# Three cross attentions: softmax sums written once, reciprocals spread by DMA, maxima in bf16 parts, loads moved

## The chip, the core and the metric

The kernel runs on one core of a Trainium2 chip. The time is device microseconds for one execution of the whole program; the number compared is the median of several executions. The engines are TensorE (PE in the profile; PEld is its weight load), VectorE (DVE), ScalarE (ACT), GpSimd (POOL) and SyncE (SP, which here only waits and starts DMAs). They run their own instruction streams and meet at semaphores.

## The reference

Four layers of a gated model on x of 8 batches x 512 tokens x 256 channels. Each layer adds a cross attention to a context of 64 tokens per batch, then another block:

```
x = x + tanh(g_xattn[i]) * cross_attention_i(layernorm(x), ctx)     # i = 0..3
x = x + tanh(g_ffn[i])   * block_i(layernorm(x))                    # local/routed attention, int8 MLP, gated unit, 8-expert MoE
```

Layers 0, 1 and 3 have a cross attention with 16 heads of 16 channels, and these three share one piece of code:

```
q = xn @ Wq + bq ; k = ctx @ Wk + bk ; v = ctx @ Wv + bv            # layer 0 rotates q and k by position
s = q k^T * scale, masked ; s = s - max(s) ; p = exp(s)
o = (p v) / sum(p) ; y = o @ Wo + bo
```

All data are fp32. Layer 2's cross attention has code of its own and isn't touched.

## The kernel before

The program is a sequence of eight stages (`L0_xattn`, `L0_ffn`, `L1_xattn`, ... `L3_ffn`). x stays in SBUF (`x_all`). Weights of the next stage are loaded by SP's queue when a stage begins: the block at `@block.sync` waits until the stage before has updated x, then starts every pair of `later.loads` (L383), then runs `early_sync_program` and the stage's own `sync_program`. The order of each engine's work is written out by hand, in `xattn_pe`, `xattn_act`, `xattn_dve` and `xattn_pool`; there is no planner.

A cross attention is a pipeline over turns n = 0, 1, ..., each holding pieces of several batches: scores of batch n, softmax of n-1, output of n-2 (`turn_of`), and in L3 also the routing for the last stage, for n-3 and n-4. Each piece is done in two halves f = 0, 1, of 8 heads. One batch of 512 queries is four tiles of 128 (t).

- `scores(n, f)` (PE, L621 for the mask, L627) writes query-major scores into banks 0 to 3; `maxima` (DVE, L1143) reduces them to 32 numbers per query row.
- `turn_max(n)` (PE, L639) transposes the maxima of a batch, in four fp32 transposes, into bank 6 (L0, L1) or 5 (L3); ACT copies them to `maxT` (`copy_max`, L905). Because bank 6 also takes the output projection, `project_out(n-2, 2)` waits for that copy.
- `scores_of_keys(n-1, f)` (PE) computes the scores again, key-major (L647), and subtracts the maxima by a matmul with a constant `minus_max` (L650), fp32; ACT takes the exponentials (`exponentials`, L901).
- `values` (PE, L660) multiplies by v into bank 4. `denominators` (PE, L671) multiplies the same exponentials by the constant `sums`: four matmuls with 32-column weights side by side (column groups), 512 columns each, into bank 5. Every sum is written 16 times, once for each channel of its head, so that it lies where the output lies.
- `normalise` (DVE) takes the reciprocal of bank 5 (L1148, 128 x 512), then multiplies bank 4 by it into `o` (L1151). `values` of the next half waits for that, as it reuses bank 4.
- `project_out` (PE, L677) and `add_out` (DVE, L1158) put the result into x.
- L0 also rotates: `partners` (PE, L608) and `rotate` (DVE, L1131, L1135, L1138). `banks_free` on PE waits until `rotate` has read its two products.

DVE's order in a turn is: maxima(n, 0); normalise(n-2, 1); statistics of later batches in turns 0 to 2; maxima(n, 1); rotate(n+1) in L0; normalise(n-1, 0); apply(n+2) (layer norm); expert choice in L3; add_out(n-2). L1 also dequantises the next stage's weights on DVE in turns 4 and 5, and runs its first layer norms in turns 7 and 8. A turn counts as steady where all pieces are present.

SP in L0 stores rows for the next stage (`units_sync`), one batch a turn, and reloads one block of them into `xn` after the third. In L3 the last 24 indirect scatters on POOL come after the loop, and the first tile of the last stage waits for all of them.

## Time and profile before

| | us |
|---|---|
| median of 3 executions | 2500.14 (2499.08 to 2505.13) |
| profiled execution | 2494.2 |
| its span, first to last instruction | 2492.2 |
| PE busy | 2329.9 |
| DVE busy | 1410.5 |
| ACT busy | 950.6 |
| POOL busy | 613.6 |

The three stages run at about 0 to 236 us (L0), 975 to 1173 us (L1) and 1660 to 1926 us (L3). Busy time is the union of an engine's instructions; matmul ends are modelled, so distances between starts are the safer measure on PE. An fp32 matmul is two records in the trace. PEclk is the granted share of TensorE's full clock. A row of windows gives the stretch and its length, then the busy time (and number of instructions) of PE, PEld, DVE, ACT and POOL, then PEclk, the mean busy share of the DMA engines, and GB/s; with a source line it has PE and PEld only. A row of groups by line ends with busy time (union) and mean ns of one instruction.

### The profile page before, as it was taken

What the parts mean: (1) busy time and instruction counts of PE and PEld (TensorE: products, weight loads), DVE (VectorE), ACT (ScalarE), POOL (GpSimd) and SP (SyncE); (2) the same over time, 40 slices, a digit from 0 to 9 for tenths busy, and PEclk for the clock granted to TensorE, in tenths of its full rate; (3) what the DMA queues carried; (4) which work ended last, traced back from release to release, by engine and by line L of the source; (5) the groups of instructions that cost most, each with busy time, mean ns of one, the idle gap of its engine ahead of it and who ended that gap; (6) DMA issues with size and microseconds to landing.
All of it is one profiled execution on the core that took longest, in us unless ns stands there. A gap on an engine that the chain in (4) does not pass through costs nothing.

```text
span 2492.2 us, 40543 instructions
## 1 busy us (share of the span) xinstructions
PE 2329.9 (93%) x15438; PEld 1656.4 (66%) x15438; DVE 1410.5 (57%) x2881; ACT 950.6 (38%) x2288; POOL 613.6 (25%) x548
## 2 busy tenths in 40 slices
PE   6997999999999998998999999988984999999998
PEld 4444677776666665444666665544553999999997
DVE  7886654674544555887466533348885444444442
ACT  1366655444444543332233322124653222222222
POOL 3234222252001002211233100014455122222222
PEclk8998999999999999999999999989996999999999
DMA  5011211121001000100001029502126222222221
GB/s 202 1 35 51 91 35 52 52 83 54 26 26 52 26 26 26 71 1 18 1 1 36 1 95 326 185 0 110 40 80 244 58 36 37 35 36 36 36 35 26
DMA packets 72087, 148.36 MB, mean 60 GB/s; under 512 B 11704, under 2 KB 59065, under 8 KB 69441
## 3 DMA queue, kind: packets, MB, share of 16 engines
q1 hardware_dynamic: 39600, 104.61, 12.3%
q0 software_dynamic: 16368, 26.23, 5.4%
q10 hardware_dynamic: 15936, 15.03, 2.1%
q8 instruction: 122, 2.00, 0.3%
q14 instruction: 61, 0.49, 0.1%
HBM read 107.42 MB, written 74.76 MB: 73 GB/s over the span
## 4 chain that ended last, share of the span: by engine, by line
PE 81%; DVE 10%; ACT 4%; issue 2%; POOL 2%; DMA 1%; SPq 0%; DVEq 0%; POOLq 0%; ACTq 0%
PE PS L2366 14%; PE PS L2392 7%; PE PS L2822 5%; PE PS L2834 5%; PE PS L1540 4%; PE PS L1531 4%; PE PS L2050 3%; PE PS L2062 3%; PE PS L2891 3%; PE PS L602 3%; PE PS L2882 3%; PE PS L2856 3%; DVE mem L1148 2%; DVE mem L1143 2%; PE PS L2927 2%
## 5 line engine op out<-in xcount | busy, mean ns | idle before, releaser
L2366 PEld LDWEIGHTS PS<-ctx2T,x_all 128*128 128x128 f32 x3124 | 361.2, 193 | 10.1 <-DVE x_all L2515 6.5
L2366 PE MATMUL PS<-ctx2T,x_all 128*128 128x128 f32 x3124 | 361.8, 276 | 5.9 <-DVE x_all L2515 5.1
L2563 POOL DMA_INDIRECT out_x<-xnT,moe_small x71 | 130.9, 1843 | 427.7 <-ACT xnT L2448 424.7
L2392 PE MATMUL PS<-mem,moe_small 128*128 x852 | 195.8, 379 | 0.8 <-ACT xnT L2448 0.8
L2515 DVE COPY x_all<-mem 128x2816 f32 x71 | 115.5, 1627 | 109.6 <-issue 96.9
L2392 PEld LDWEIGHTS PS<-mem,moe_small 128*128 128x128 f32 x852 | 156.4, 190 | 19.4 <-issue 1.2
L1148 DVE RECIPROCAL mem<-PS 128x512 f32<-128x512 f32 x48 | 160.9, 3351 | 11.3 <-PE PS L671 11.0
L1143 DVE TENSOR_REDUCE mem<-PS 128x32 f32<-128x2048 f32 x48 | 109.9, 2289 | 50.8 <-PE PS L627 50.7
L3208 DVE TENSOR_REDUCE moe_small<-PS 128x2 f32<-128x1024 f32 x64 | 78.5, 1226 | 99.2 <-PE PS L2882 99.2
L3353 POOL TENSOR_TENSOR mem<-mem,moe_small 128x512 f32<-128x512 f32 x64 | 82.2, 1304 | 207.5 <-DVE moe_small L3218 207.4
L3032 ACT ACTIVATE mem<-PS,moe_small 128x128 f32<-128x128 f32 x256 | 89.9, 377 | 94.2 <-DVE moe_small L3203 94.2
L2891 PEld LDWEIGHTS PS<-consts,mem 128*128 128x128 f32 x768 | 87.8, 141 | 54.3 <-issue 52.4
L3041 ACT ACTIVATE mem<-PS,moe_small 128x512 f32<-128x512 f32 x128 | 86.9, 690 | 85.0 <-DVE moe_small L3208 85.0
L677 PE MATMUL PS<-mem 128*128 128x256 f32 x384 | 100.5, 407 | 19.7 <-DVE mem L1151 12.5
L1540 PE MATMUL PS<-mem 128*128 128x256 f32 x512 | 116.6, 381 | 0.0
L2528 DVE TENSOR_TENSOR moe_small<-PS,moe_small 128x128 f32<-128x128 f32 x71 | 20.7, 292 | 167.1 <-ACT moe_small L2441 167.1
L2782 POOL DMA_INDIRECT mem<-routed_out,moe_small x32 | 30.8, 962 | 342.1 <-DMA routed_out<-mem 334.6
L1531 PE MATMUL PS<-mem 128*128 128x512 f32 x256 | 113.9, 594 | 0.0
L901 ACT ACTIVATE mem<-PS,mem 128x2048 f32<-128x2048 f32 x32 | 63.0, 1967 | 117.6 <-PE PS L650 117.6
L1540 PEld LDWEIGHTS PS<-mem 128*128 128x128 f32 x512 | 95.5, 190 | 18.5 <-issue 7.0
L677 PEld LDWEIGHTS PS<-mem 128*128 128x128 f32 x384 | 73.8, 203 | 44.4 <-issue 23.3
L2891 PE MATMUL PS<-consts,mem 128*128 128x128 f32 x768 | 101.1, 275 | 0.9 <-DVE mem L3226 0.9
(382 smaller groups left out, 4596.9 us busy)
## 6 DMA issues: line engine op xcount, KB each, us to landing
slots<-in_trash_rows SPq DMA_DIRECT2D x8, 4290.0 KB, 63.8
mem<-in_L_ffn_experts SPq DMA_DIRECT2D x8, 2176.0 KB, 13.6
xn<-slots ACTq DMA_DIRECT2D x53, 130.0 KB, 2.1
x_all<-in_x SPq DMA_DIRECT2D x8, 512.0 KB, 8.1
xn<-unit_rows SPq DMA_DIRECT2D x8, 512.0 KB, 4.5
mem<-unit_rows SPq DMA_DIRECT2D x8, 512.0 KB, 4.3
out_x<-x_all ACTq DMA_DIRECT2D x8, 512.0 KB, 2.9
unit_rows<-moe_small SPq DMA_DIRECT2D x7, 512.0 KB, 3.2
```

The source lines that it names most:

```text
L677: last = nc.tensor.matmul(PS[:, BANK_M + 1 - t // 2, (t % 2) * D:(t % 2 + 1) * D], s.o[:, b % 2, f, t * P:(t + 1) * P], s.wo[:, f, :], sta ...
L1143: dve.tensor_reduce(s.max.rearrange("p (g n) -> p g n", g=G)[:, :, 8 * f:8 * f + 8], PS[:, 0:G, :].rearrange("p g (a k) -> p g a k", k=SC) ...
L1148: dve.reciprocal(s.recip, PS[:, BANK_DEN, :]).then_inc(s.sems["recip_ready"], 1)
L1531: last = nc.tensor.matmul(PS[:, 2 + n % 2, :], s.w1[:, k, n * P:(n + 1) * P], s.hT[:, k, :], start=k == 0, stop=k == KD - 1)
L1540: last = nc.tensor.matmul(PS[:, 6 + t % 2, 0:D], s.yT[:, n, t * P:(t + 1) * P], s.w2[:, n, :], start=n == 0, stop=n == KF - 1)
L2366: last = nc.tensor.matmul(PS[:, moe_bank(j, part), c * P:(c + 1) * P], m.w[:, j % 2, k, at:at + P], m.rowT[:, j % 2, k, :], start=k == 0, ...
L2392: last = nc.tensor.matmul(PS[:, MOE_BANK_Y, 0:D], m.hT[:, j % 2, n, :], w[:, :, at:at + D], start=n == 0, stop=n == KE - 1)
L2515: dve.tensor_copy(m.w[:, j % 2, :, :].rearrange("p k n -> p (k n)"), s.experts[:, bass.ds(expert, 1), 0:KD * WIDE].rearrange("p o n -> p ( ...
L2563: nc.gpsimd.indirect_dma_start(s.T["out"], bass.IndirectOffsetOnAxis(s.token[:, j % 4:j % 4 + 1], 0), m.result[:, j % 4, :], None, compute ...
L2822: last = nc.tensor.matmul(PS[:, BANK[p.heavy, "k", j], :], s.wk[p.heavy][:, k, m * P:(m + 1) * P], columns(p, j)[:, k, :], start=k == 0, s ...
L2834: last = nc.tensor.matmul(PS[:, BANK[p.heavy, "v", j], t * P:(t + 1) * P], columns(p, j)[:, k, t * P:(t + 1) * P], s.wv[p.heavy][:, k, m * ...
L2891: last = nc.tensor.transpose(PS[:, BANK_PT + h, n * P:(n + 1) * P], s.probs[:, par, h, n * P:(n + 1) * P], e.ident)
```

## The change

1. `denominators`: for all batches but the last, a sum is written for each query tile t into one of the 16 rows of its head, over 128 columns instead of 512. That takes 16 matmuls of 128 columns with the constants `sums_of_tile[:, t, :]`, accumulating over t. The reciprocal is then 128 x 128. The last batch keeps the old form.
2. SP stores these reciprocals to DRAM (128 rows of 512 bytes), waits for the store, and reads them back broadcast: each of the 16 rows of a head gets the head's 512 numbers, into `s.recip`. One buffer serves all halves, so each read waits for the product before it.
3. ACT copies the values' bank to `o` (`copy_o`, two a turn), and DVE multiplies `o` in place one slot later: half 0 after the next turn's first maxima, half 1 after its second maxima. `values` of the next half now waits for ACT's copy.
4. The maxima are split by DVE into three bf16 parts (`split_max`, four operations on 64 elements per row), transposed in bf16 into bank 4, copied as bf16, and subtracted by bf16 matmuls with 12 rows of `minus_max`. The projection no longer waits for that copy, and its tiles stand together around `turn_max`.
5. Loads: in L1 ACT starts the next stage's loads, in turns 2 to 5; in L3 SP starts two experts' loads and a third one after the last reciprocals; in L0 ACT stores the unit rows and SP reloads `xn` after the last reciprocals. DVE's dequantisation in L1 moves to turns 6 and 7. In L0 POOL adds the bias ahead of scaling the next stage's weights.

```diff
+def split_max(eng, order, s, b):
+    eng.wait_ge(s.sems["max_ready"], 2 * (b + 1))
+    order.mark(eng.tensor_copy(max_part(s, 0), s.max))
+    order.settle()
+    order.mark(eng.tensor_tensor(s.max_rest, s.max, max_part(s, 0), ALU.subtract))
+    order.settle()
+    order.mark(eng.tensor_copy(max_part(s, 1), s.max_rest))
+    order.settle()
+    eng.tensor_tensor(max_part(s, 2), s.max_rest, max_part(s, 1), ALU.subtract).then_inc(s.sems["max_split"], 1)
+
+def spread_recips(sp, s, b, f):
+    k = KD * b + f
+    few = s.recips[f].rearrange("(q r) n -> q r n", r=HD)[:, 0:TB, :].rearrange("q t n -> q (t n)").rearrange("q (o n) -> q o n", o=1)
+    sp.wait_ge(s.sems["recip_ready"], k + 1)
+    sp.dma_start(s.recips[f], s.recip_few).then_inc(s.sems["recip_stored"], 16)
+    sp.wait_ge(s.sems["recip_stored"], 16 * (k + 1))
+    wait_for(sp, s.sems["o_ready"], k)
+    sp.dma_start(s.recip, few.broadcast_to([NH // KD, HD, S])).then_inc(s.sems["recip_spread"], 16)
+
+def recips_sync(sp, e, s):
+    for b in range(B - 1):
+        for f in range(KD):
+            spread_recips(sp, s, b, f)
+    if s.late_loads:
+        for dst, src in s.next.loads:
+            sp.dma_start(dst, src).then_inc(s.next.weights_loaded, 16)
+        sp.dma_start(*s.next.expert_loads[5]).then_inc(s.next.expert_loaded_s[3], 16)
...
     def turn_max(b):
-        pe.wait_ge(s.sems["max_ready"], 2 * (b + 1))
+        pe.wait_ge(s.sems["max_split"], b + 1)
+        if b == 0:
+            pe.wait_ge(s.sems["v_ready"], B)
+        else:
+            pe.wait_ge(s.sems["o_copied"], KD * (b - 1) + 1)
...
     def values(b, f):
-        wait_for(pe, s.sems["o_ready"], KD * b + f)
+        wait_for(pe, s.sems["o_copied"], KD * b + f)
+        if f == 1:
+            pe.wait_ge(s.sems["maxT_ready"], min(b + 2, B))
...
     def denominators(b, f):
+        if b == B - 1:
...
+        else:
+            for t in range(TB):
+                for c in range(G):
+                    last = nc.tensor.matmul(PS[c * GR:(c + 1) * GR, BANK_DEN, 0:P], s.sums_of_tile[:, t, :],
+                                            s.probsT[:, f, c, t * P:(t + 1) * P], start=t == 0, stop=t == TB - 1)
...
-            if old and not s.front:
-                project_out(n - 2, 0)
         if before:
             scores_of_keys(n - 1, 1, min(2 * n + 2, 2 * B))
         if s.rope:
             banks_free()
         if route:
             logits(n - 3)
-        if old and s.front:
+        if old:
             project_out(n - 2, 0)
+            project_out(n - 2, 1)
         if now:
             turn_max(n)
...
+    def copy_o(b, f):
+        act.wait_ge(s.sems["pv_psum"], KD * b + f + 1)
+        wait_for(act, s.sems["y_psum"], 2 * (b - 1))
+        nc.scalar.activation(s.o[:, b % 2, f, :], PS[:, BANK_O, :], ACT.Copy).then_inc(s.sems["o_copied"], 1)
...
+    def reciprocals(b, f):
+        dve.wait_ge(s.sems["den_psum"], KD * b + f + 1)
+        if b == B - 1:
+            dve.wait_ge(s.sems["o_ready"], KD * b + f)
+            dve.reciprocal(s.recip, PS[:, BANK_DEN, :]).then_inc(s.sems["recip_ready"], 1)
+        else:
+            wait_for(dve, s.sems["recip_stored"], 16 * (KD * b + f))
+            dve.reciprocal(s.recip_few, PS[:, BANK_DEN, 0:P]).then_inc(s.sems["recip_ready"], 1)
...
     def normalise(b, f):
-        dve.tensor_tensor(s.o[:, b % 2, f, :], PS[:, BANK_O, :], s.recip, ALU.mult).then_inc(s.sems["o_ready"], 1)
+        dve.wait_ge(s.sems["o_copied"], KD * b + f + 1)
+        if b == B - 1:
+            dve.wait_ge(s.sems["recip_ready"], KD * b + f + 1)
+        else:
+            dve.wait_ge(s.sems["recip_spread"], 16 * (KD * b + f + 1))
+        o = s.o[:, b % 2, f, :]
+        dve.tensor_tensor(o, o, s.recip, ALU.mult).then_inc(s.sems["o_ready"], 1)
...
         if old:
-            normalise(n - 2, 1)
+            reciprocals(n - 2, 1)
+            if n - 2 < B - 1:
+                normalise(n - 2, 0)
...
             maxima(n, 1)
-        if early and n == 4:
+        if old:
+            normalise(n - 2, 1)
+        if now:
+            split_max(dve, order, s, n)
+        if early and n == 6:
...
         if before:
-            normalise(n - 1, 0)
+            reciprocals(n - 1, 0)
+            if n - 1 == B - 1:
+                normalise(n - 1, 0)
```

## Rows read from the trace of the kernel before

**Rows 1.** The page, parts 1 and 4: engines' busy time; shares of the chain.

```profile
PE 2329.9 (93%) x15438; PEld 1656.4 (66%) x15438; DVE 1410.5 (57%) x2881; ACT 950.6 (38%) x2288; POOL 613.6 (25%) x548
...
PE 81%; DVE 10%; ACT 4%; issue 2%; POOL 2%; DMA 1%; SPq 0%; DVEq 0%; POOLq 0%; ACTq 0%
```

**Rows 2.** Windows, a turn of L0, L1, L3: length, busy, PEclk, DMA share, GB/s.

```profile
107.30:129.50 22.20, 21.10 (x180) 10.92 (x177) 18.88 (x19) 10.35 (x23) 6.09 (x11) 1.00 0.01 3
1052.00:1072.30 20.30, 19.27 (x173) 10.03 (x174) 15.46 (x15) 6.80 (x7) 2.37 (x1) 1.00 0.00 1
1776.40:1798.40 22.00, 21.82 (x193) 13.30 (x193) 19.57 (x49) 14.54 (x24) 12.98 (x15) 1.00 0.21 74
```

**Rows 3.** Timeline of PE, L0: start, us, engine, line, operation, operands, records.

```profile
110.89 0.40 PE L621 MATMUL PS<-mem 1*128 1x512 bf16 x4
111.11 1.06 PE L627 MATMUL PS<-mem 32*128 32x128 f32 x32
112.10 1.98 PE L608 MATMUL PS<-mem,consts 128*128 128x512 f32 x4
114.02 1.07 PE L660 MATMUL PS<-mem 128*32 128x512 f32 x8
114.90 1.04 PE L671 MATMUL PS<-mem 128*32 128x512 f32 x8
...
116.83 1.04 PE L650 MATMUL PS<-mem 32*128 32x512 f32 x8
117.80 0.75 PE L639 MATMUL PS<-consts,mem 128*128 128x128 f32 x4
118.39 1.89 PE L677 MATMUL PS<-mem 128*128 128x256 f32 x8
```

**Rows 4.** Windows, source L2902; groups by line, weight loads of L671.

```profile
315.25:316.30 1.05, 1.04 (x16) 0.85 (x16) 1.00 1.05 380
...
L671 PEld LDWEIGHTS PS<-mem 128*32 128x32 f32 x384 | 13.5, 116 | 31.6 <-issue 31.6
```

**Rows 5.** Timeline of DVE, the same turn of L0.

```profile
112.25 2.29 DVE L1143 TENSOR_REDUCE mem<-PS 128x32 f32<-128x2048 f32 x1 [3.01 <-PE PS L627]
...
118.12 3.35 DVE L1148 RECIPROCAL mem<-PS 128x512 f32<-128x512 f32 x1
121.58 0.69 DVE L1151 TENSOR_TENSOR mem<-PS,mem 128x512 f32<-128x512 f32 x1
...
123.47 1.65 DVE L1158 SCALAR_TENSOR_TENSOR x_all<-PS,tg,x_all 128x256 f32<-128x256 f32 x4
```

**Rows 6.** Timeline of DVE in a turn of L3: one small operation.

```profile
1789.46 0.23 DVE L1209 TENSOR_TENSOR moe_small<-consts,moe_small 128x64 f32<-128x64 f32 x1
```

**Rows 7.** One line's instructions: the rotary sum, minimum, median, maximum in ns.

```profile
L1138 DVE TENSOR_TENSOR mem<-mem x8: 1225/1226/3236, 28.6 to 183.4; 128x1024 f32<-128x1024 f32 x8
```

**Rows 8.** DMA issues of L1: KB each, median us to landing.

```profile
mem<-in_L_ffn_sc SPq DMA_DIRECT2D x2, 1024.0 KB, 10.0
routed_out<-mem SPq DMA_DIRECT2D x1, 256.0 KB, 2.1
...
mem<-in_L_xattn_wv SPq DMA_DIRECT2D x1, 256.0 KB, 3.2
```

**Rows 9.** Chain of waits, early turns of L0 and L3: start, us, what.

```profile
77.60 1.94 PE PS L660 x8
...
1739.48 2.09 PE PS L647 x8
```

**Rows 10.** Timeline of PE, last turns of L0 and of L1.

```profile
208.84 1.14 PE L647 MATMUL PS<-mem 32*128 32x512 f32 x8
...
228.56 6.14 PE L677 MATMUL PS<-mem 128*128 128x256 f32 x16 [4.37 <-DVE mem L1151]
...
1148.64 1.14 PE L647 MATMUL PS<-mem 32*128 32x512 f32 x8
...
1167.40 5.38 PE L677 MATMUL PS<-mem 128*128 128x256 f32 x16 [3.75 <-DVE mem L1151]
```

121 lines of the change are left out of this document (66 added, 55 removed).

## The prediction

> **What bounds the kernel now.** I read the page first: PE is busy 93% of the span and holds 81% of the chain that ended last, DVE 10% [rows 1]. Time taken from VectorE is worth something only where it releases TensorE; time taken from TensorE is worth its own length where no other chain steps in. So I cut a window of one steady turn from each of the three stages that the diff touches [rows 2]: L0 22.2 us with PE busy 21.1 and DVE 18.9; L1 20.3, 19.3, 15.5; L3 22.0, 21.8, 19.6. PE bounds a turn, with 1.1, 1.0 and 0.2 us idle, and DVE is close behind. The other stages aren't touched. The profiled execution lasts 2494.2 us (span 2492.2), 6 us under the median 2500.1; I make the sum against it and carry the difference to the median.
>
> **TensorE's work in one turn.** The timeline of PE gives prices, as distances from start to start [rows 3].
> - The fp32 matmuls that subtract the maxima (L650) take 0.97 us for four row groups. The nearest row in bf16 is L621, four row groups of 512 columns: 0.22 us until L627 starts. Two sets in a turn, -1.5 us; bounds -1.5 and 0 (bf16 no faster).
> - The four transposes of the maxima (L639) take 0.59 us; in bf16 I take 0.25, bounds 0.1 and 0.59: -0.3.
> - The sums: 4 matmuls of 512 columns become 16 of 128, so 8 weight loads of 32 columns become 32. L671 takes 1.04 us now. L2902, 16 loads and matmuls of 128 columns in two column groups, takes 1.05, 0.064 us each [rows 4]; in four groups half of that, 32 x 0.032 = 1.05. Upper bound: loads one behind the other at their own length, 116 ns for L671's, 32 x 0.116 = 3.7 us. But that row has 384 loads in 13.5 us of busy time, 35 ns each: the four groups load side by side. I take 1.1 us, so +0.1 for the two sums of a turn.
>
> Net -1.7 us of PE in a turn. A rule speaks against the last point: by "TensorE: Matmul & The Clock Gate" of the Trainium skill (part 3, the mechanism) a weight load overlaps running matmuls only when the row group differs, and column groups all span the same 128 rows. The two-group row, 64 ns for a load and a matmul together, contradicts it so far; it stays as a rival.
>
> **VectorE, and what is late next.** A full reciprocal is 3.35 us [rows 5]; a quarter of its columns I put at 0.9 (bounds 0.84, a quarter, and 1.2). 4.9 us a turn leave. Four operations on 64 elements or fewer enter, each waiting for the one before; one costs 0.23 [rows 6]: 1.0 us. The product stays at 0.69 or falls to 0.6. DVE's sum ends near 15 us in L0, 12 in L1, 16 in L3, so its order matters now, not its sum. I count from the end of a turn's second scores on PE.
> - L0: the delayed product and the split (1.6 us) now stand ahead of the rotary step, and PE's output projection waits until that step has read its banks. Maxima 2.3 [rows 5] + 1.6 + 2 x 1.23 for the cosine and sine products (1024 elements each time, priced by the rotary sum [rows 7]) = 6.4 us. PE arrives after partners 1.9, values 0.9, sums 1.0 [rows 3], shifted scores 0.97 + 0.22 = 5.0. Stall 1.4. The old 1.1 us of waits go: the maxima no longer use the banks of the projection, and ACT has room (busy 10.4 of 22.2 [rows 2]). 21.1 - 1.7 + 1.4 = 20.8 of 22.2: **-1.4**.
> - L1: half a projection moves from ahead of the second shifted scores to behind them. PE has only values and sums, 1.9 us, to cover maxima of 2.3 with their hand-offs: stall 0.5. 19.3 - 1.7 + 0.5 = 18.1 of 20.3: **-2.2**.
> - L3: the routing transposes still give that cover. 21.8 - 1.7 + 0.1 = 20.2 of 22.0: **-1.8**. DVE's chain over expert choice and ranks brings the next maxima about when PE asks for them; below 20 us there is nothing more.
> - ACT gains two copies of about 0.6 us a turn ahead of the exponentials. I put them at 0, hidden by ACT's idle time; in L3 (busy 14.5 of 22.0 [rows 2]) they may cost 0.6 in a turn if that cover is gone.
>
> **The transfers.** SP stores 64 KB, waits, then loads 256 KB. A 256 KB store lands in 2.1 us, a 256 KB load in 3.2, loads of 1 MB in 10 [rows 8]. I take 5.5 us for the round trip, bounds 4.5 and 12. The first of a turn starts after the small reciprocals of f = 0 and is needed after projection's adds, the next maxima and reciprocals, by the same counting 6.4 us later in L0 and 7 in L1. The second has 8 us (5 in L3), and PE asks for its result 2.5 us later still. So the round trip is covered up to about 8 us. Queued behind it on SP: the reload of xn for the next stage (now after turn 8, with some 25 us in hand) and L3's expert loads, three at about turn 8 and four when the stage ends, against the scatters that start the last stage. L1's weights move to ACT's queue, a megabyte at a time, and may delay one round trip in a turn. All this at 0; if the experts come late, 5 to 10 us once.
>
> **Turns that aren't steady** (estimates, by following the order above through each).
> - Turns 0 to 2. The values of f = 1 waited for the normalised output of f = 0 and then ran slowly: L660 takes 1.94 us where rows 3 have 1.07; in L3 the shifted scores come late and take 2.09 [rows 9]. They now wait for ACT's copy: L0 -5, L1 -4, L3 -5. Turn 0 pays 1 us for the split and for waiting on the values' banks in L1 and L3; in L0 it is paid back by the bias add, which moves away from the rotary sum that once took 3.24 us instead of 1.23 [rows 7]. L0 -5, L1 -3, L3 -4.
> - Turns 6 and 7 go by chains of maxima, exponentials and scores. A turn gives 2 x 0.75 in bf16, in L1 also the wait for the copied maxima, in L3 the 2.5 us of reciprocal ahead of each second maxima: L0 -2.5, L1 -4.3, L3 -6.
> - From the shifted scores of batch 7 to the last projection: L0 19.7 us, L1 18.8 [rows 10]. Now the last spread product is done 6.8 us after these scores start (reciprocals 1, transfers 5.2, product 0.6), and the full reciprocals stand behind it. L0: 6.8 + 3.35 + 0.69 + adds 1.65 [rows 5] + 3.35 + 0.69 = 16.5, **-3.2**, since values no longer wait for the normalised output. L1 is bound by DVE there, with the next stage's norms in the same queue: its product was done after 3.35 + 0.69 + 0.1 = 4.2, now after 6.8, **+2.5**. L3 as L0, -3.2.
>
> **Sum.** L0: 5 + 4 steady turns x 1.4 + 2.5 + 3.2 = 16.3. L1: 3 + 4 x 2.2 + 1 (its weights' dequantisation leaves two steady turns) + 4.3 - 2.5 = 14.6. L3: 4 + 3 x 1.8 + 6 + 3.2 = 18.6. Together 49.5. New hand-offs between engines in 24 turns at about 0.15 us: -3.6. Gain 46: 2494.2 - 46 = 2448 for a profiled execution, 2500.1 - 46 = **2454 us** for the median.
>
> **Rivals.**
> 1. The transfers come late, and the products with them. For: two dependent transfers per half turn, and 10 us where megabytes are in flight [rows 8]. Against: DMA moves 3 GB/s in the L0 turn and 1 in L1's [rows 2]. Beyond 8 us each microsecond costs one in each of some 20 turns: at 9 us 2474.
> 2. The weight loads of the sums aren't hidden; this is the slower case. Place: PE, 14 sums in a stage, 42 in all. Price at 116 ns per load: 3.7 - 1.05 = 2.6 us, x 42 = 110, less the gain of 46: 2500 + 64 = 2564. It decides from 46 / 42 = 1.1 us more per sum, 67 ns per load and matmul where I have 33. For: nothing in this kernel loads 32 columns for 128. Against: the 35 and 64 ns of rows 4. The page named above would have it go this way.
> 3. TensorE falls to the lower of its clocks inside steady turns, as before the 6.14 us projection [rows 10]. For: PE's wait in L0 grows to 1.4 us in one piece. Against: L1's turn with 1.0 idle shows 1.00 [rows 2]. A fifth of the turns with 5 us at half clock: about 2476.
> 4. The unsteady turns give nothing: 4 x 1.4 + 4 x 2.2 + 3 x 1.8 = 20, 2480.
>
> **How the numbers follow.** Forecast (gain 28 to 64) 0.60; rivals 1, 3, 4 and mixtures (gain 8 to 28) 0.22; over 64, 0.05; no change 0.06; slower 0.07, mostly rival 2. About 0.3% (7.5 us) is what a measurement can tell from no change. Faster 0.87, same 0.06, slower 0.07. The likeliest case alone has 2436 to 2472; leaving out two in ten I give 2434 to 2488.
>
> **What would show it.** The bf16 set at 0.2 to 0.3 us; sums near 1.05 us in 32 matmuls; small reciprocals at 0.85 to 0.95; the spread landing within 6 us of them; steady turns of 20.8, 18.1 and 20.2; in L0 a wait of 1.4 us before the projection; L1 later from its last shifted scores on. Wrong if sums take 2 us, if DVE waits for a transfer and PE behind it, or if the granted clock in those turns is under 1.00.

## The result: 20 us faster, less than half of the forecast

The changed kernel takes 2484.1 us (2480.9 to 2488.7, four runs) beside 2502.6 us (2499.1 to 2506.2) for the kernel before in the same session (one chip, one stretch of time): ratio 0.9924, 95% interval 0.9912 to 0.9936. Two repeats gave 0.9932 (0.9919 to 0.9944) and 0.9909 (0.9894 to 0.9923). The gain is 17 to 23 us where 46 were forecast; the time lies inside the range, near its upper end. The profiled execution took 2488.7 us (span 2486.7).

Page of the changed kernel, parts 1 and 4, against [rows 1]: TensorE lost 25 us of busy time and VectorE 74, and the span only 5.5. But the trace of [rows 1] is of an execution of 2494.2 us, 8 below the median of 2502.6. Two profiles from one session, before_again and after_third (below), have spans of 2502.9 and 2483.3 us and 2332.2 and 2298.8 us of busy TensorE: of 33 us of work that left TensorE, 20 left the span.

```profile
PE 2305.1 (93%) x16254; PEld 1672.7 (67%) x16254; DVE 1336.4 (54%) x2977; ACT 978.5 (39%) x2336; POOL 613.6 (25%) x548
...
PE 79%; DVE 9%; ACT 4%; issue 3%; POOL 2%; DMA 2%; another core or an unknown queue 0%; SPq 0%; DVEq 0%; ACTq 0%; POOLq 0%
```

Windows of one steady turn of L0, L1 and L3, columns as in [rows 2]: 21.35, 18.05 and 20.57 us where those had 22.20, 20.30 and 22.00, at full clock. Its other steady turns of L0 take 20.97 and 20.45.

```profile
142.06:163.41 21.35, 19.39 (x220) 11.35 (x217) 17.39 (x22) 15.13 (x37) 8.17 (x14) 1.00 0.16 57
1045.50:1063.55 18.05, 17.41 (x217) 10.68 (x213) 11.15 (x18) 8.13 (x9) 2.35 (x1) 1.00 0.26 97
1742.20:1762.77 20.57, 20.36 (x237) 13.72 (x233) 15.16 (x49) 15.24 (x26) 5.12 (x7) 1.00 0.18 59
```

TensorE's timeline in that turn of L0, against [rows 3]: sums (L737) in 32 records, the bf16 subtraction (L711), the bf16 transposes (L699), and the wait for the rotary step.

```profile
149.71 1.06 PE L737 MATMUL PS<-mem 128*32 128x128 f32 x32
150.70 1.14 PE L708 MATMUL PS<-mem 32*128 32x512 f32 x8
151.66 0.39 PE L711 MATMUL PS<-mem 32*128 32x512 bf16 x4
153.19 1.99 PE L744 MATMUL PS<-mem 128*128 128x256 f32 x8 [1.14 <-DVE mem L1204]
155.03 0.39 PE L699 MATMUL PS<-consts,mem 128*128 128x128 bf16 x4
155.25 1.95 PE L744 MATMUL PS<-mem 128*128 128x256 f32 x8
```

The starts 149.71 and 150.70 are 0.99 us apart, L699 to the next L744 0.22. Groups by line answer to [rows 4, 5]: the small reciprocal takes 0.95 us, a weight load of the sums 112 ns, and 1344 of them keep the load path busy for 39.3 us, 29 ns each. They are hidden, as the prediction priced them.

```profile
L1222 DVE RECIPROCAL mem<-PS 128x128 f32<-128x128 f32 x42 | 39.9, 951 | 3.5 <-PE PS L737 2.3 <-remote 0.9 <-DMA recips<-mem 0.2
L737 PEld LDWEIGHTS PS<-mem 128*32 128x32 f32 x1344 | 39.3, 112 | 28.7 <-issue 27.2 <-DVE mem L1222 1.4
```

**Where the gain went.** Each cross-attention stage is cut in three: from its keys to the query of batch 3 (start), to the query of batch 7 (four steady turns), and to the first product of the next stage, for L3 to the end of the kernel (drain). Two pairs of profiles, each pair from one session; the second pair is without the scatters (below). Microseconds, changed minus before. The row "sums" adds up each row above it over the three stages: all starts, all steady parts, all drains. The steady part of L3 was predicted for three turns:

```
                    predicted     after_third            no_scatter
                                  - before_again         - before_no_scatter
starts  L0 L1 L3    -5 -3 -4      -9.4 +4.8 +1.0         -0.8 +2.7 +3.9
steady  L0 L1 L3    -5.6 -9.8 -5.4   -4.3 -10.2 -4.5     -4.9 -10.2 -10.0
drains  L0 L1 L3    -5.7 -1.8 -9.2   +0.9 +2.1 -0.2      +1.5 +3.2 -2.6
sums                -12 -20.8 -16.7  -3.6 -19.0 +2.8     +5.8 -25.1 +2.0
spans                             2502.9 to 2483.3       2483.3 to 2461.5
```

The steady turns together give about what they should, the drains nothing, and the starts together nothing that repeats. What lies between these parts differs by +0.2 us in the first pair and -4.5 in the second. Two things have to be read with the table:

- The steady part of L3 holds four intervals, and the first of them, from the query of batch 3 to that of batch 4, fell from 23.3 to 19.3 us (24.7 to 19.0 in the second pair). The three turns behind it gave only 0.4 us in the first pair and 4.2 in the second, for 5.4 predicted. That -19.0 lies so near to -20.8 is partly luck.
- One part of the same kernel differs between its profiles. In after, after_again and after_third the start of L1 takes 63.7, 56.8 and 63.6 us (57.0 and 58.8 in before and before_again), the drain of L0 58.1, 60.7 and 61.8 (62.0 and 60.9), the drain of L1 64.8, 63.3 and 63.1 (58.6 and 61.1). In all of these profiles, and in the pair without the scatters, the change makes the start of L0 shorter, and the start of L3 and the drain of L1 longer. A few microseconds in the start of L1 or the drain of L0 of a single profile show little.

### The profile page after: what moved, and what is told of

Read it like the earlier page. It is cut to its first block, busy times and chain, and to the rows that moved or that the text cites. A ratio compares the mean times of both kernels' runs of the same rounds, so it can differ in the third digit from the quotient of the medians.

```text
span 2486.7 us, 42502 instructions
## 1 busy us (share of the span) xinstructions
PE 2305.1 (93%) x16254; PEld 1672.7 (67%) x16254; DVE 1336.4 (54%) x2977; ACT 978.5 (39%) x2336; POOL 613.6 (25%) x548
## 4 chain that ended last, share of the span: by engine, by line
PE 79%; DVE 9%; ACT 4%; issue 3%; POOL 2%; DMA 2%; another core or an unknown queue 0%; SPq 0%; DVEq 0%; ACTq 0%; POOLq 0%
PE PS L2457 14%; PE PS L2483 7%; PE PS L2913 5%; PE PS L2925 5%; PE PS L1632 5%; PE PS L1623 4%; PE PS L2142 3%; PE PS L2154 3%; PE PS L2982 3%; PE PS L2973 3%; PE PS L662 3%; PE PS L744 3%; PE PS L2947 3%; DVE mem L1212 2%; PE PS L3018 2%
## 5 line engine op out<-in xcount | busy, mean ns | idle before, releaser
L744 PE MATMUL PS<-mem 128*128 128x256 f32 x384 | 107.7, 433 | 26.9 <-DVE mem L1231 20.7
L1632 PE MATMUL PS<-mem 128*128 128x256 f32 x512 | 116.6, 381 | 0.0
L744 PEld LDWEIGHTS PS<-mem 128*128 128x128 f32 x384 | 79.7, 217 | 51.3 <-issue 24.2
L2619 DVE TENSOR_TENSOR moe_small<-PS,moe_small 128x128 f32<-128x128 f32 x71 | 20.7, 291 | 167.6 <-ACT moe_small L2532 167.6
L1632 PEld LDWEIGHTS PS<-mem 128*128 128x128 f32 x512 | 95.4, 190 | 18.6 <-issue 7.0
L662 PE MATMUL PS<-xnT,mem 128*128 128x512 f32 x192 | 92.5, 627 | 6.5 <-ACT xnT L944 6.5
L2913 PE MATMUL PS<-xnT,mem 128*128 128x512 f32 x192 | 96.4, 625 | 0.8 <-ACT xnT L3098 0.8
```

What stands on the lines that cost most here:

```text
L662: last = nc.tensor.matmul(PS[:, BANK_M + f, :], s.wq[:, k, f * P:(f + 1) * P], e.xnT[:, k, :], start=k == 0, stop=k == KD - 1)
L744: last = nc.tensor.matmul(PS[:, BANK_M + 1 - t // 2, (t % 2) * D:(t % 2 + 1) * D], s.o[:, b % 2, f, t * P:(t + 1) * P], s.wo[:, f, :], sta ...
L1632: last = nc.tensor.matmul(PS[:, 6 + t % 2, 0:D], s.yT[:, n, t * P:(t + 1) * P], s.w2[:, n, :], start=n == 0, stop=n == KF - 1)
L2913: last = nc.tensor.matmul(PS[:, BANK[p.heavy, "k", j], :], s.wk[p.heavy][:, k, m * P:(m + 1) * P], columns(p, j)[:, k, :], start=k == 0, s ...
```

## Experiments

**1. Does it repeat, and is it the exposed spread, the bank, or the spread as a whole?** Three edits beside the changed kernel.

after_again: no edit.

> The changed kernel itself once more, with a second profile. Theory A (the gain of the steady turns is real and is given back in the turns that are not steady: a wait in turn 0, the exposed spread of batch 6, and half clock behind both): the ratio to the kernel before is again near 0.9924 (0.991 to 0.994); the profile has again a wait of 4 to 6 us of TensorE ahead of the first transposes of the maxima in L1_xattn and L3_xattn, and waits of 4 to 8 us of VectorE for the spread of batch 6. The stalls put down to no work of this core (one turn of L3_xattn that took 25.8 us, a VectorE pause of 4.1 us at the start of L1_xattn) are chance and will be elsewhere or absent. Theory B (the steady turns themselves are disturbed, by transfers or by POOL beside VectorE): the 25.8 us turn comes back at the same place.

Measured 2484.2 beside 2503.6 us, 0.9932. The turn of 25.8 us came back at the same place (25.75), as theory B has it, so it isn't chance. Of theory A's rows most held: VectorE waited 6.4 us for the spread of batch 6 in L0, 2.8 and 3.7 in L1, 7.1 in L3, and TensorE 4.7 us ahead of the first transposes of the maxima in L3. In L1 TensorE waited there 1.6 us and not 4 to 6; VectorE's pause of 4.1 us at that place was absent, and the start of L1 was 6.9 us shorter.

last_two_full: the full form for the last two batches.

```
-    if b == B - 1:            # sums, reciprocal, product
+    if b >= B - 2:
-for b in range(B - 1):        # spread by transfers
+for b in range(B - 2):
```

> Batch 6 as well as batch 7 uses the full sums and a 128x512 reciprocal with no transfer, in all three stages. Theory A: VectorE's waits for the spread of batch 6 (5.5 us in L0_xattn, 2.9 and 3.9 in L1_xattn, 7.3 in L3_xattn) go and two reciprocals of 3.36 us take the place of two of 0.95 in each stage; net 2 to 3 us in L0, 3 to 4 in L1 and L3 with the clock that comes back: 8 to 11 us faster than the changed kernel, ratio near 0.989. Theory B (disturbed steady turns): 0 to 3 us, since turn 7 gains 2.4 us of VectorE time and loses nothing else. Theory C (the tail is set by the last batch's own chain of sums, 3.36 us reciprocal and projection): nothing.

Measured 0.9924 (0.9911 to 0.9937): a miss for A. VectorE's timeline in the drain of L1, first the changed kernel (after_third), then this one:

```profile
1135.96 0.69 DVE L1231 TENSOR_TENSOR mem<-mem 128x512 f32<-128x512 f32 x1 [2.77 <-DMA mem<-recips]
1140.62 0.69 DVE L1231 TENSOR_TENSOR mem<-mem 128x512 f32<-128x512 f32 x1 [3.96 <-DMA mem<-recips]
...
1144.57 3.36 DVE L1219 RECIPROCAL mem<-PS 128x512 f32<-128x512 f32 x1
```

```profile
1130.38 2.28 DVE L1723 SCALAR_TENSOR_TENSOR mem<-mem 128x2048 f32<-128x2048 int32 x1
...
1134.90 3.36 DVE L1224 RECIPROCAL mem<-PS 128x512 f32<-128x512 f32 x1
...
1140.54 3.35 DVE L1224 RECIPROCAL mem<-PS 128x512 f32<-128x512 f32 x1
...
1147.95 3.36 DVE L1224 RECIPROCAL mem<-PS 128x512 f32<-128x512 f32 x1
```

The waits of 2.77 and 3.96 us are gone, but from 1126.7 to 1160.7 us VectorE has no gap: the reciprocals, the next stage's norms and its weight conversion (L1723, which the change moved here from turn 5) fill it. The drain takes 62.2 us for 63.1, that of L0 61.3 for 61.8. One wait was traded for about the same length of work: in L1 the last projection comes 20.7 us behind the first shifted scores of batch 7 for 25.9, but these scores come 35.6 us behind the query of batch 7 for 32.3.

first_in_m: the maxima of batch 0 into the old bank.

```
-PS[:, BANK_O, ...]    pe.wait_ge(v_ready, B) if b == 0
+PS[:, BANK_O if b else BANK_M, ...]    (turn_xn(2) waits for the copy)
```

> The maxima of batch 0 alone are transposed into the bank that the kernel before used for them, so that they don't wait until all token values are placed. Theory A: in turn 0 of L1_xattn and L3_xattn TensorE starts them 1.8 us earlier (the length of the placing behind the split); the rest of the 4.7 and 5.7 us waits is VectorE's own queue of layer-norm statistics ahead of the second maxima, and stays. 3 to 5 us over three stages, ratio near 0.991. Theory B: the same place gives nothing, because TensorE then waits for the layer norm of batch 2: ratio 0.9924.

Measured 0.9933 (0.9921 to 0.9946): nothing, as B has it.

no_spread: full sums and reciprocals for all batches.

```
+SPREAD = {"L0": 0, "L1": 0, "L3": 0}      (7, 7, 0 in l3_full below)
-    for b in range(B - 1):
+    for b in range(SPREAD[s.name[:2]]):
-        if b == B - 1:
+        if b >= SPREAD[s.name[:2]]:
```

> All batches use the full sums and the 128x512 reciprocal with no transfer; the bf16-part maxima, the copies of the values on ScalarE and the later product stay. By the steps of the prediction: VectorE gets 4.8 us a turn more than in the changed kernel. In L1_xattn (TensorE-bound, VectorE 10.8 of 18.05 us) the steady turn stays at 18.0 to 18.3 us; in L0_xattn and L3_xattn VectorE is at 18.9 and 19 to 20 us a turn again, with the rotary step waiting, and the turns go from 20.6 to 21.5 to 22.5. Theory A then: 5 turns by 1.5 in L0 and L3 lost, 8 to 10 us won in the drains: about as fast as the changed kernel, 0.991 to 0.995. Theory B (transfers disturb): faster than it, 0.989 or less. If the spread is what carries the gain: 0.996 to 1.0.

Measured 1.0048 (1.0032 to 1.0064), 29 us slower than the changed kernel by the two ratios; only the "spread is what carries the gain" branch points that way, and by less. L1's turn was to stay at 18.0 to 18.3 us and took 19.3, L0's was to take 21.5 to 22.5. Windows of a turn of L0, L1, L3:

```profile
129.55:155.37 25.82, 20.77 (x173) 10.21 (x169) 22.34 (x23) 15.12 (x37) 8.55 (x13) 0.95 0.06 21
1071.31:1090.61 19.30, 17.46 (x168) 9.42 (x165) 15.93 (x19) 8.13 (x9) 2.39 (x1) 1.00 0.14 56
1796.35:1817.56 21.21, 20.73 (x188) 12.69 (x184) 19.97 (x53) 15.37 (x26) 13.34 (x15) 1.00 0.22 76
```

L0's turn is 25.8 us with VectorE busy 22.3, and the kernel is slower than the one before: the split, the copies and the late product only pay where the reciprocal is short.

**2. The size of the bf16 term, and the stages one by one.**

f32_maxima: no split, fp32 transposes and subtraction, everything else as changed.

```
-        nc.tensor.transpose(... columns of max_parts, bf16 identity)
+        nc.tensor.transpose(... columns of max, e.ident)
-        nc.tensor.matmul(PS[:, g, :], minus_max, maxT[r, b % 2, :], ...)   (bf16)
+        nc.tensor.matmul(PS[:, g, :], minus_max, maxT[r, :], ...)          (fp32)
```

> The changed kernel with the maxima kept as in the kernel before: no split on VectorE, fp32 transposes and an fp32 subtraction on TensorE; sums, spread and late loads stay. By the prediction's steps TensorE pays 1.5 + 0.3 us a turn again and VectorE is 0.85 us a turn shorter. In L1_xattn, where TensorE sets the turn, the steady turn goes from 18.05 to 19.7 us (+1.65). In L0_xattn, where the rotary step on VectorE comes last, it gains back 0.85 and loses part of 1.7: 20.5 to 21.5 us. L3_xattn as L1: +1 to +1.7. Over 24 turns +25 to +35 us against the changed kernel, ratio 1.003 to 1.007. Rival: if the bf16-part maxima aren't what moved the turns (VectorE's latency sets them and the split costs what the subtraction saves), the turns stay and the ratio is 0.992 to 0.995.

Measured 0.9978 (0.9965 to 0.9992), outside both branches. The L1 turn is 19.53 us, 1.48 more than 18.05 (predicted 1.65):

```profile
1049.32:1068.85 19.53, 18.89 (x225) 11.58 (x221) 10.41 (x14) 8.11 (x9) 2.37 (x1) 1.00 0.25 89
```

The starts of L0, L1, L3 take 69.7, 58.5 and 61.1 us where after_third has 67.3, 63.6 and 62.1, the drains 62.1 and 63.3 where it has 61.8 and 63.1, so the whole came to 14 us (0.9978 against 0.9924) and not 25 to 35. The start of L1 is to be held against after_again (56.8), which like this profile has no late signal there (experiment 3). L0's four steady turns take 83.3 us for 84.3: there the bf16 maxima give nothing. L3's take 91.1 for 88.0.

l3_full: spread in L0 and L1 alone.

> Full sums and the 128x512 reciprocal without transfers in L3_xattn alone; L0_xattn and L1_xattn as in the changed kernel. The kernel without any spread had uniform turns of 21.2 us in L3_xattn and took 820.8 us from the keys of L3_xattn to the end, against 824.1 and 827.1 us in the two profiles of the changed kernel and 824.4 in the kernel before. Theory A (the spread gives nothing in L3_xattn, since what it frees on VectorE is lost in two late turns and in the drain): 3 to 6 us faster than the changed kernel, ratio near 0.991, and the slow turn of 25.8 us is gone. Rival (the better L3_xattn of that kernel came from its later arrival or its other state of memory traffic): the stage takes 824 us or more and the ratio stays at 0.9925.

Measured 0.9914 (0.9898 to 0.9931), but L3 from its keys on took 827.8 us: the rival's condition. The ratio alone doesn't tell the rival from theory A. The turns of 21.2 us were there, with 23.7 in turn 3.

weights_early: the loads of L1_ffn all in turn 2, conversion in turns 4 and 5.

```
-if s.act_loads and 2 <= n < 6:   (one load a turn)
+if s.act_loads and n == 2:       (all)
-if early and n in (6, 7): ffn1_weights(..., n - 6)
+if early and n in (4, 5): ffn1_weights(..., n - 4)
```

> The loads of L1_ffn are all issued by ScalarE in turn 2 of L1_xattn, and its weights are converted on VectorE in turns 4 and 5 as in the kernel before, not in 6 and 7. Theory A (in the drain of L1_xattn VectorE has no gap, so the 2.63 us of the second conversion in turn 7 and part of the first are on the path): the time from the last query of L1_xattn to the first product of L1_ffn goes from 63.3 to 60 us, 2.5 to 4 us in all, ratio 0.9915. Rival (the four transfers of 1 MB issued at once delay the spread of the reciprocals in turns 2 and 3 by their 10 us, and a product waits for it): nothing or 2 to 5 us slower.

Measured 0.9896 (0.9879 to 0.9912), the lowest ratio of all versions that do the whole work. The drain of L1 fell from 63.1 to 61.9 us, half of what was expected, and its turns 4 to 6 rose by 0.2 to 0.5 where the spreads met the conversion. The rest of its lead is in L3, which the edit doesn't touch (turn 5 takes 22.5 us for 25.1).

**3. The late signals.** In every profile of the changed kernel and its variants so far ScalarE and VectorE had waits of 1 to 4 us put down to no work of the core ("remote"), mostly at the same places; the trace of before that the prediction rests on has none. pe_pad shifts TensorE's program by 128 waits that are already met.

```
+    for _ in range(129 if s.name[:2] == "L0" else 1):
         pe.wait_ge(s.keys_loaded, 16 * len(s.first_loads))
```

> 128 more instructions that do nothing (waits that are already met) at the start of TensorE's program in L0_xattn. In every profile with the new sums there are short stretches in which ScalarE, VectorE and GpSimd get TensorE's signals 1 to 4 us late, at the same places each time (the border of the two halves of L0_ffn, turns 4 and 5 of L3_xattn), and the kernel before has none. Theory P (TensorE's instruction stream: its program grew, and a block of instructions comes late at these places): the places move, the turn of 25.8 us in L3_xattn is shorter or another one is long, and the loss of 1.3 us at the border in L0_ffn changes. Theory Q (something fixed in the schedule, as the first scattered rows beside the spread): the same places with the same lengths. Time: within 6 us of the changed kernel either way.

Measured 0.9935 (0.9919 to 0.9952); turns of 24.96 and 23.23 us in L3 and the same places: no sign of P, though the number of fetched instruction blocks didn't change either, so the shift may have been too small to count.

no_scatter and before_no_scatter: the two kernels without the indirect DMAs that scatter the rows to their slots; the semaphore is incremented in their place.

```
-            nc.gpsimd.indirect_dma_start(m.T["slots"], ...).then_inc(m.scattered_s[b % Y_BUFS], 16)
+            pool.sem_inc(m.scattered_s[b % Y_BUFS], 16)
```

> The changed kernel without the 64 indirect DMAs by which GpSimd scatters the routed rows in L3_xattn (the later expert stage works on rows that were never written; no other work is left out). In all profiles so far the signals of TensorE that come 1 to 4 us late are released 0.7 to 1.2 us behind the last of a group of these DMAs, on GpSimd (1771.56 against 1772.27 us, 1804.27 against 1805.48, 1875.30 against 1876.36). Theory S (a signal that falls into a group of indirect DMAs waits for its end): the slow turns of L3_xattn (25.8 and 22.5 us) fall to the 20.5 us of the turn before them, no late signal is left in L3_xattn, and the stage from its keys to the first product of the experts is 8 to 14 us shorter. Rival Q (the memory traffic of the spread, or the order of the turn, makes them slow): the turns stay above 22 us.

> The kernel before without the same 64 indirect DMAs. Theory S: its turns of 21.9 to 22.0 us have the group of five DMAs end at 1814.35 us, behind the wait that matters (1813.97), so they stay within 0.5 us of 22.0, and only the drain gets up to 3 us shorter: the late signals are a cost that only the shorter turn has. Rival: the kernel before gains as much from leaving them out as the changed one (8 us or more), and then they don't explain the missing gain. Its other stages are a second profile of the kernel before: L0_xattn 223 to 227 us from its keys, L1_xattn 196 to 200.

The kernel before ran at 2493.3 us here, 10 less than in the other sessions. no_scatter 0.9884 (0.9866 to 0.9902), before_no_scatter 0.9970 (0.9956 to 0.9985), their medians 21.5 us apart. No late signal is left in either. The window of the turn that took 25.8 us, and the same turn of before_no_scatter:

```profile
1758.09:1778.66 20.57, 20.36 (x236) 13.73 (x233) 15.45 (x53) 15.24 (x26) 5.15 (x7) 1.00 0.18 59
```

```profile
1774.41:1796.42 22.01, 21.84 (x197) 13.31 (x193) 19.57 (x50) 14.55 (x24) 5.12 (x7) 1.00 0.08 25
```

But another run of that session, warm_weights (below), has its scatters and no late signal either, with turns of 20.56 to 20.58. So the session was the difference, and theory S isn't shown. after_third and before_again test that side by side.

> The changed kernel, beside the kernel before on one chip. Theory C (late signals belong to the chip): where the kernel before runs at about 2493 us, the changed kernel runs at 2470 to 2476 us, has no late signal, and its turns in L3_xattn are 20.6 us; where the kernel before runs at 2503 us, the changed one is at 2484 with the late signals and turns of 22.5 and 25.8 us. The ratio is 0.992 to 0.993 either way. Rival (they come with the changed kernel): late signals and 2484 us beside 2493.

> The kernel before, with a second profile. Theory C: on a chip on which it runs at 2503 us its profile has the late signals too, and turns of L3_xattn above 22.5 us; on one with 2493 us none. Rival: none on either.

The kernel before ran at 2504 us; both profiles have late signals. VectorE's second addition in turn 6 of L3, in before_again (the releaser's name is a guess of the profile) and in after_third, each behind the last indirect DMA of a group on GpSimd:

```profile
1817.47 0.96 POOL L1397 DMA_INDIRECT slots<-mem,moe_small  x1 [0.30 <-issue]
...
1819.63 0.88 DVE L1158 SCALAR_TENSOR_TENSOR x_all<-PS,tg,x_all 128x256 f32<-128x256 f32 x2 [1.97 <-DMA unit_rows<-moe_small]
```

```profile
1821.34 0.96 POOL L1488 DMA_INDIRECT slots<-moe_small  x1 [0.30 <-issue]
...
1823.54 0.88 DVE L1238 SCALAR_TENSOR_TENSOR x_all<-PS,tg,x_all 128x256 f32<-128x256 f32 x2 [2.01 <-remote]
```

1.20 and 1.24 us behind the end of that DMA's issue, in both kernels. The late signal at the start of L1 stands behind a group of indirect gathers instead:

```profile
984.64 0.95 POOL L2873 DMA_INDIRECT mem<-routed_out,moe_small  x1 [0.30 <-issue]
...
986.58 2.29 DVE L1212 TENSOR_REDUCE mem<-PS 128x32 f32<-128x2048 f32 x1 [4.09 <-remote]
```

The two profiles of the changed kernel that have it take 63.7 and 63.6 us for that start, after_again without it 56.8. Theory C holds as far as late signals come to both kernels and don't explain the missing gain: without any, the kernels were 21.5 us apart and not 46. Nor had the trace of [rows 1] any, whose 2494.2 us are near the session at 2493.3. Theory C said "the chip", and that isn't shown: chip number 13 had three of the sessions, two at 2505 us with late signals and the one at 2493.3 without, and whether that was one piece of silicon isn't recorded. In L3 they cost more in the changed kernel: turns 4 to 6 take 20.6, 25.1, 23.0 for 21.9, 23.6, 23.6, so that 0.4 us is left there of the 4.2 that the pair without scatters shows.

**4. Starts and drains, one wait at a time.**

starts: fewer statistics in turn 0 of L0 and L1, and first_in_m.

```
-{0: (2, 3, 4), 1: (5, 6), 2: (7,)}   # batches whose statistics stand in turn n
+{0: (2,), 1: (3, 4), 2: (5, 6, 7)}
```

> In L0_xattn and L1_xattn only the statistics of batch 2 stand in turn 0 on VectorE (3 and 4 in turn 1, 5 to 7 in turn 2, as L3_xattn has it), and the maxima of batch 0 go to the bank that doesn't wait for the token values. Theory V (VectorE's queue sets the start): the second maxima of batch 0 start 3.9 us earlier and TensorE's wait of 5.7 us ahead of their transposes falls to under 2; the first three turns of L1_xattn go from 46 to 50 us down to 43 to 46, L0_xattn gains 1 to 3 us; 3 to 6 us in all, ratio 0.990 to 0.991. Rival (what is late next is the layer norm of batch 2 and the copies on ScalarE, and turn 1 gets the statistics instead): within 2 us of the changed kernel.

Measured 0.9968 (0.9957 to 0.9979): 13 us slower than the changed kernel beside it. The wait did go. TensorE in the start of L1, after_third and then starts:

```profile
1002.49 0.59 PE L699 MATMUL PS<-consts,mem 128*128 128x128 bf16 x4 [5.64 <-DVE mem L1194]
```

```profile
1005.67 0.39 PE L697 MATMUL PS<-consts,mem 128*128 128x128 bf16 x4 [0.19 <-DVE mem L601]
```

and that start got 3.9 us shorter (59.7 for 63.6, both with a late signal of 4.1 us there; after_again, without one, waits 1.6 us at the same transposes and takes 56.8). But turn 3 of L0 grew from 21.1 to 26.9 us, the start of L1_ffn stands 7.0 us later than in after_third (1169.4 for 1162.4) and the last query of L3 11.9 us (1818.5 for 1806.6).

warm_weights: weights_early, and matmuls that nothing reads ahead of the last projection.

```
+def keep_busy():   # called before project_out(B - 1, 0) waits
+    for _ in range(9): nc.tensor.matmul(PS[:, 3, :], e.ident, s.probsT[:, 1, 0, :], start=True, stop=True)
```

> weights_early with 9, 12 and 9 matmuls of 128x512 that nothing reads, on TensorE ahead of its last wait for the product of batch 7 in L0_xattn, L1_xattn and L3_xattn. They take 4.0 to 5.4 us at full clock, inside waits of 4.4, 5.2 to 6.1 and 4.4 us. Theory H (the drain of each stage is paid at half clock because TensorE stood idle): the last projection takes 3.7 us in place of 5.4, 6.7 and 6.2, and the stage behind starts at full clock: 5 to 8 us in all, ratio 0.9865 to 0.988. Rival (the clock falls all the same, or what comes behind waits for VectorE's normalisation anyway): within 2 us of weights_early, 0.9896.

Measured 0.9921 (0.9908 to 0.9935): a miss, since nine of them took 7.99 us and not 4.0 (9, 12 and 9 in L0, L1 and L3). short_warm has 4, 5 and 4.

> weights_early with 4, 5 and 4 matmuls that nothing reads ahead of the last projections; in the run before this one 9 of them took 8.0 us (0.89 us each, not the 0.45 that had been counted), longer than the wait, and the projection started 3.5 us late but took 3.62 us in place of 5.4. Now they take 3.6, 4.4 and 3.6 us inside waits of 4.4, 5.2 to 6.1 and 4.4 us. Theory H: each last projection takes 3.7 us, at full clock, and starts when the product is there: 1.7, 2.5 and 2.5 us, and 3 to 4 us of weights_early; ratio 0.986 to 0.989. Rival (too short to hold the clock, or what comes behind pays it): as weights_early.

Measured 0.9904 (0.9885 to 0.9924). TensorE at the end of L0, after_third and then short_warm (L743 is the burst, L750 the projection):

```profile
216.31 6.34 PE L744 MATMUL PS<-mem 128*128 128x256 f32 x16 [4.37 <-DVE mem L1231]
```

```profile
216.57 3.70 PE L743 MATMUL PS<-mem,consts 128*128 128x512 f32 x8
220.92 3.72 PE L750 MATMUL PS<-mem 128*128 128x256 f32 x16 [0.65 <-DVE mem L1237]
```

The idle time costs 2.6 us in the projection behind it, as H says (granted clock 0.58 in the first projection's window, 1.00 in the second's). The drains take 59.4 and 59.9 us, 2.4 and 3.2 less, of which weights_early alone has 1.2 in L1. In L0 that isn't outside the changed kernel's own 58.1 to 61.8, and the drain and L0_ffn together take 801.8 us for 800.4 to 801.6. The whole isn't told apart from weights_early.

late_projection: the projection of batch 6 behind the values and sums of batch 7, its addition behind their product.

```
 values(n - 2, 1); denominators(n - 2, 1)
+if n == B + 1: project_out(B - 2, 0..3)        (not in turn B)
+if n == B + 1: add_out(n - 3)                  (VectorE, after normalise)
```

> The changed kernel with the projection of batch 6 on TensorE placed behind the values and the sums of batch 7, second half, and its addition on VectorE behind their reciprocal and product, in L0_xattn and L1_xattn. Theory O (TensorE stands in order behind the spread of batch 6): the 2.1 us wait and 5.3 us of projection leave the chain in L0_xattn, and the projection fills the later wait of 4.4 us and holds the clock: the time from the last query to L0_ffn goes from 61.8 to 55 to 57 us, in L1_xattn from 63.1 to 58 to 61: 7 to 10 us in all, ratio 0.988. Rival D (VectorE's own queue sets the drain: it waits for the spread, then two reciprocals of 3.36 us): no more than 2 us in either, ratio 0.991 to 0.992.

Measured 0.9912 (0.9898 to 0.9927). The drain of L0 takes 58.6 us for 61.8 in after_third and 58.1 in after, that of L1 61.5 for 63.1: neither reaches O's numbers, and L1's is D's size. Then the first norm of L0_ffn waited for GpSimd, which still had the unit rows of the last batches to do. From there to the keys of L1 it takes 747.2 us for 739.8, and with the drain 805.8 for 800.4 to 801.6 in the three profiles of the changed kernel:

```profile
229.47 0.16 DVE L3244 TENSOR_TENSOR moe_small<-moe_small 128x4 f32<-128x4 f32 x1 [6.67 <-POOL moe_small L3428]
```

combined: the two edits above, late_projection and short_warm, in one kernel.

> late_projection together with short_warm (the loads of L1_ffn in turn 2, its conversion in turns 4 and 5, and the short bursts ahead of the last projections). Theory O: the bursts in L0_xattn and L1_xattn are then mostly taken over by the projection of batch 6 and may cost up to 4 us each; L3_xattn keeps its 1 to 2. If both add: ratio 0.985 to 0.987; if the bursts now delay the last projection: 0.988 to 0.991, later than late_projection with weights_early would be.

Measured 0.9922 (0.9904 to 0.9939), drains 64.7 and 63.6 us: the bursts now delay the projection, the worse branch. With first_in_m and fewer statistics in turn 0 of L1 added (combined_l1) 2 to 4 us less were expected; it came to 0.9914 (0.9900 to 0.9929), 2 us less and within the noise.

## Why the prediction was wrong, step by step

- **TensorE's work in one turn**: right but for one price. Sums stand 0.99 us from the next row (1.1 predicted), transposes 0.22 (0.25). A bf16 set takes 0.32 to 0.36 for 0.22: it was priced by L621, which has one row in each group where the set has 32. f32_maxima prices the whole bf16 term at 1.48 us in a turn of L1 for 1.5 + 0.3. Rival 2 is out: loads take 112 ns and are hidden. The rule of the Trainium skill that the prediction named ("TensorE: Matmul & The Clock Gate", part 3) would have made it slower by 64 us and doesn't hold for these column groups.
- **VectorE**: right. Reciprocal 0.95 (0.9), split 0.85 (1.0), the rotary wait in L0 1.14 (1.4).
- **The transfers**: right in the steady turns; no steady turn of L1 waits for them. In turn 8 nothing covers them; the 6.8 us that the prediction counted there are the term that failed most, see below.
- **Steady turns**: 20.5 to 21.4, 18.05, 20.57 for 20.8, 18.1, 20.2. Together -19.0 and -25.1 for -20.8, partly by luck (see the table).
- **Turns that aren't steady: the step that failed.** They were to give 28.7 of the 49.5 us; starts and drains together gave 0.8 in one pair and lost 7.8 in the other. The term that missed most is the one "from the shifted scores of batch 7 to the last projection". It had -3.2, +2.5 and -3.2 us in L0, L1 and L3. From before_again to after_third it measures +2.1 (18.2 to 20.3), +7.1 (18.8 to 25.9) and -0.1 (27.0 to 26.9), and without the scatters +2.5, +7.0 and -1.2: 13 and 12 us of the 26 and 24 by which the gains fall short. The 19.7 us of L0 that the sum set out from were long, too: the two other profiles of the kernel before have 18.2.

  The sum had the last spread product done 6.8 us after these scores start. In after_third that took 9.7 us in L1, 8.6 in L0 and 11.5 in L3. In L1 SP's queue does a store, a read, a store and a read (the products of 1135.96 and 1140.62 are shown under last_two_full):

```profile
1130.60 0.32 SPq L609 DMA_DIRECT2D recips<-mem  x1
1131.64 1.14 PE L708 MATMUL PS<-mem 32*128 32x512 f32 x8
1132.16 0.60 SPq L612 DMA_DIRECT2D mem<-recips  x1
1133.22 0.32 SPq L609 DMA_DIRECT2D recips<-mem  x1
1136.73 0.60 SPq L612 DMA_DIRECT2D mem<-recips  x1
...
1154.96 2.42 DVE L1231 TENSOR_TENSOR mem<-mem 128x512 f32<-128x512 f32 x1
...
1157.52 5.08 PE L744 MATMUL PS<-mem 128*128 128x256 f32 x16 [6.12 <-DVE mem L1231]
```

  One buffer serves both halves, so the second read is issued behind the first product, 3.5 us after its store, where the first read followed its store by 1.56. From the last spread product on VectorE has no gap up to the projection: the 2.9 us that the product is late and the 1.7 us by which the last product is stretched (2.42 for 0.69, beside GpSimd; see the end of the document) are together the 4.6 us that L1 missed. The same place in L0, on TensorE, VectorE and SP's queue:

```profile
196.03 1.14 PE L708 MATMUL PS<-mem 32*128 32x512 f32 x8
198.73 0.61 SPq L612 DMA_DIRECT2D mem<-recips  x1
199.44 0.40 SPq L898 DMA_DIRECT2D xn<-unit_rows  x1
203.98 0.69 DVE L1231 TENSOR_TENSOR mem<-mem 128x512 f32<-128x512 f32 x1 [5.80 <-DMA mem<-recips]
204.82 5.27 PE L744 MATMUL PS<-mem 128*128 128x256 f32 x16 [2.16 <-DVE mem L1231]
210.02 1.06 PE L723 MATMUL PS<-mem 128*32 128x512 f32 x8
212.01 3.36 DVE L1219 RECIPROCAL mem<-PS 128x512 f32<-128x512 f32 x1 [1.01 <-PE PS L733]
```

  The sum let VectorE alone set the pace here. But values and sums of batch 7 stand on TensorE behind the projection of batch 6, which waits 2.16 us for the spread and then runs in 5.27 (granted clock 0.70). In the profile after, where it runs in 3.69 at 1.00, the whole takes 18.6 us. Taking the spread out of batch 6 (last_two_full) brings the term to 18.3, 20.7 and 22.6 us, but the full reciprocals then stand ahead of it, and the drains of L0 and L1 got only 0.5 and 0.9 us shorter.

  In turn 0, where the sum had 1 us in L1 and L3 and nothing in L0, TensorE waits 4.0, 5.6 and 4.0 us ahead of the first transposes of the maxima (after_third; 1.6 in L1 in after_again), for 1.8, none and 2.2 in before_again.

  What these have in common: I shortened one chain at a time by the length of the work taken out. There several chains stand within a few microseconds of each other: VectorE's queue of statistics, the spread, the next stage's norms and conversion, GpSimd's unit rows. Experiments that removed one got little of it: 0.9 us of 6.7 in the drain of L1 in last_two_full, 1.2 of 2.6 in weights_early, 3.9 of 5.5 in starts (and more lost in L0), 1.6 in L1 in late_projection, with more lost in L0_ffn. And TensorE falls to half clock more often in the drain of L1. Windows of the drains of L0 and L1, before_again and then after_third:

```profile
175.29:236.17 60.88, 49.37 (x372) 26.38 (x369) 42.99 (x38) 41.25 (x114) 20.25 (x43) 0.94 0.13 44
1116.47:1177.52 61.05, 50.06 (x376) 27.00 (x373) 44.83 (x57) 16.81 (x13) 8.60 (x5) 0.92 0.00 1
```

```profile
161.82:223.62 61.80, 48.30 (x449) 28.90 (x445) 37.05 (x46) 44.74 (x120) 23.04 (x48) 0.89 0.21 71
1099.31:1162.44 63.13, 45.99 (x453) 27.49 (x449) 41.58 (x68) 20.74 (x19) 8.60 (x5) 0.89 0.09 27
```

  The granted clock is 0.89 for 0.94 and 0.92. In L1 that repeats (0.84, 0.84 and 0.89 in the three profiles of the changed kernel, 0.97 and 0.92 in before and before_again), in L0 it doesn't (0.97, 0.92 and 0.89 for 0.92 and 0.94).
- **Loads at 0**: partly wrong. Placing L1_ffn's loads late put 2.6 us of conversion on VectorE into turn 7, in a drain where it has no gap. The reload of xn in L0 is issued 0.7 us behind the last read of reciprocals (above), two expert loads 0.6 us behind that of L3:

```profile
1853.42 0.58 SPq L612 DMA_DIRECT2D mem<-recips  x1
1854.05 0.95 SPq L622 DMA_DIRECT2D mem<-in_L_ffn_experts  x2
1860.10 0.69 DVE L1231 TENSOR_TENSOR mem<-mem 128x512 f32<-128x512 f32 x1 [6.84 <-DMA mem<-recips]
```

  From the issue of these two reads to the product it takes 5.2 to 5.4 and 6.7 to 7.2 us in the three profiles of the changed kernel, for 3.6 to 4.4 at every other read that VectorE waits for. That the loads behind them lengthen them is likely and not shown: no run takes them away.
- **Rival 4** (the unsteady turns give nothing, 2480) is what happened. It stood inside a chance of 0.22 with two other rivals and mixtures; after a sum of which 58% came from estimates of such turns it deserved the larger half.

What stays open: why signals come late in most sessions and not in all, which chain sets the starts of L0 and L3, whether the late loads lengthen the last spread, and what the other half of the missing gain, in the starts and in turns 6 and 7, consists of. No version was shown to beat the changed kernel; weights_early (0.9896) is the nearest to it, with an interval that meets that of 0.9909; the changed kernel didn't run in its session.

## What to carry to other kernels

Credit a saving in full only in turns whose bound you have read from a window, and in starts and drains with nothing until the second and third chain there are read too; a saving on an engine that already waits comes back as idle time, and on TensorE at half clock. When a transfer replaces work inside a pipeline, look at the last turn, where no other work is left to cover it, and count there how often its one buffer is used in a row. Take a profile of the kernel before in the same session as that of the changed one before trusting a difference of 10 us.

## What the runs showed of the hardware

- The same kernel before took 2493.3 us in one session and 2502.6 to 2505.3 in the five others with the changed kernel or its variants. The one had no late signals in its three profiles, the others had them in all sixteen, in both kernels, in the rows shown above 1.0 to 1.2 us behind the last of a group of indirect DMAs on GpSimd. The profile of 2494.2 us behind [rows 1] has none.
- VectorE's operations with two operands in SBUF stretch while GpSimd runs a tensor operation of 128x1024: the rotary sum takes 2.90 us in the L0 turn for 1.23 [rows 7], the product 2.42 to 2.46 for 0.68, also at the end of L1 where TensorE waits for it. They end as if they only began when GpSimd's ended: the sum 1.08 us behind it (156.15 for 155.06), the product of 141.42 0.55 behind it (143.88 for 143.33). Beside GpSimd's operation of 128x8 that takes 1.67 us (L1467) the product stays at 0.63.
- 32 weight loads of 32 columns in four column groups cost 0.99 us with their matmuls, though one takes 112 ns.
